# Cross attention over a long context: both batches' 32 heads in one pipeline, values read from DRAM by groups of four heads

## The chip, the cores and the metric

The program runs on one core of one Trainium2 chip. The metric is device time in microseconds (us) from start to end of one execution; less is better.

## What is computed

The program is a stack of twelve attention and feed-forward blocks on `x` of 2 batches x 256 tokens x 256 channels. Two of them, L0_xattn and L1_xattn, attend to a long context, `ctx_1024`, of 2 x 4096 x 256. Both have 16 heads of 16 channels and compute, per batch and head, softmax(q k^T / 4) v over all keys, then an output projection, and add the result to `x`:

```python
# L0_xattn: keys and values are the context rows as they are, and 256 projected rows of fside
q = x1 @ Wq + bq
k = concat([ctx, fside @ Wk + bk]);  v = concat([ctx, fside @ Wv + bv])      # 4352 rows each
# L1_xattn: keys and values are projections of the context
q = x1 @ w_q.T + b_q;  k = ctx @ w_k.T + b_k;  v = ctx @ w_v.T + b_v         # 4096 rows each
out = softmax(q @ k.T / 4) @ v @ Wo + bo
```

Scores are computed to float32 accuracy from bfloat16 products: q and k are each written as a sum of three bfloat16 parts, and six products of parts are stacked on 96 rows of one matmul. Three more rows carry the negated row maximum.

## The kernel before, in words

Every block is a row of *stages* (`stage`): in each, the five engines run their own instruction streams, ordered by semaphores, and all engines meet at a stage's end. `cross_attention` handles both blocks, `raw` for L0_xattn. It first loads weights and the context of batch 0 and clears a value tensor `V` of 128 x key tiles x 512 floats (32 columns for each head: 16 values, a 1 for the sum of weights, zeros). Then come `normalize`, and `store_parts` for the queries, which makes products in PSUM, splits each tile of 128 x 512 into three bfloat16 parts (ScalarE makes the first, VectorE the rest, ScalarE the second, VectorE the third) and sends them to a DRAM scratch tensor through SyncE's DMA queue.

A hardware loop `turns` runs twice, once for each batch: load the stacked queries `qS`; fill `V` (for L0 by GpSimd copies of the context, for L1 by 32 projected tiles in `gemms`); `store_parts` for the keys (L0: 16 tiles turned by TensorE and 2 projected; L1: 16 projected); `long_attention` for 16 heads; a small stage `kept` that copies the result. Within `long_attention` SyncE loads the keys of one head into one of three buffers `kst`, six pieces of 16 partitions and one row group of ones; the loads for head i are issued when the scores of head i-3 are done:

```python
for i in range(N):
    if i >= 3:
        sp.wait_ge(score_ready, (i - 2) * per_head)
    for dst, src in key_loads(i):
        sp.dma_start(dst, src).then_inc(keys[i % 3], 16)
    if i == 2:
        for dst, src in next_loads: ...           # the context of batch 1
```

TensorE's order is written out by hand: in units of up to four key tiles it interleaves products for maxima of a later head (`maximum`, `psA`), scores of this head (`score`, `psS`), and values (`values`, `psO`). VectorE takes row maxima (L593), and GpSimd splits the negated maxima into three bfloat16 parts (`split_maxima`, L409 to L412), which TensorE turns (`turn`, L554) and VectorE copies under the queries (L603). The first score of head h waits for that. ScalarE exponentiates (L651). The first maximum of head i waits for `keys[i % 3]`. A head has 9 units in L0 and 8 in L1. The maxima run one head and four units ahead of the scores, so a head's maxima are all taken some 8 us after the head before it began.

## Time and profile before

| | us |
|---|---|
| median of 3 runs (lowest, highest) | 3368.19 (3364.87, 3373.6) |
| the profiled execution's own time | 3367.49 |
| its span in the trace | 3365.6 |
| TensorE busy (matmul) | 2692.3, 80% |
| VectorE, ScalarE, GpSimd busy | 1671.1, 1130.9, 191.8 |
| L0_xattn, from its first load to the next block's | 15.38 to 676.95 |
| L1_xattn, the same | 1209.56 to 1868.08 |

The page of the profile gives busy time of each engine, forty slices of the span with the granted TensorE clock, DMA queues, and the costliest groups of instructions. "SPq" is SyncE issuing DMAs, so its times are those of issue. "Granted clock" is TensorE's, as a share of 2.4 GHz. In stretches ("windows") the DMA share is the mean busy share of 16 DMA engines; it is modelled and can pass 1.

### The profile page before, as it was taken

The numbers are of one execution on the slowest core, as the hardware profiler recorded it, in microseconds if no ns is written. First come the engines' busy times: TensorE is split into PE (matmuls) and PEld (weight loads), VectorE is DVE, ScalarE is ACT, GpSimd is POOL, SyncE is SP. The second block draws the span as 40 slices with busy tenths as digits, with TensorE's granted clock in tenths as the row PEclk, the third lists the DMA queues.
The fourth block names the chain that finished last, engine by engine and source line by source line (L and its number), as shares of the span: only waits on it lengthen the run. The fifth ranks groups of instructions, "written<-read, shape, count | busy, mean of one in ns | idle before, by whom it ended". The sixth has DMA issues, their size and how long they took to land. (4 is left out here: it accounts for less than half of the span.)

```text
span 3365.6 us, 40011 instructions
## 1 busy us (share of the span) xinstructions
PE 2692.3 (80%) x15192; PEld 1516.4 (45%) x15192; DVE 1671.1 (50%) x2588; ACT 1130.9 (34%) x2060; POOL 191.8 (6%) x362
## 2 busy tenths in 40 slices
PE   3799499878999967998798489596773759978777
PEld 2344244435555543445344255343222646747446
DVE  5677477422111136783686487333897223221423
ACT  2466366511111103773476145121321213312220
POOL 2000100000000000000000055000000000000000
PEclk8799699988999987999799656797776889978888
DMA  4632553121222125441642000100100331020200
GB/s 156 148 61 44 118 107 59 25 77 38 75 75 75 37 88 154 69 59 38 153 63 40 24 10 1 48 24 0 51 0 0 125 137 51 1 78 1 82 0 7
DMA packets 89495, 202.15 MB, mean 60 GB/s; under 512 B 10770, under 2 KB 66322, under 8 KB 78354
## 3 DMA queue, kind: packets, MB, share of 16 engines
q1 hardware_dynamic: 85566, 184.09, 22.1%
q10 hardware_dynamic: 3750, 15.65, 1.2%
q8 instruction: 115, 1.88, 0.2%
q14 instruction: 64, 0.52, 0.1%
HBM read 171.56 MB, written 28.15 MB: 59 GB/s over the span
## 5 line engine op out<-in xcount | busy, mean ns | idle before, releaser
L593 DVE TENSOR_REDUCE sta_parts<-sta_psA 128x1 f32<-128x1024 f32 x544 | 626.1, 1188 | 220.4 <-PE sta_psA L513 216.8
L651 ACT ACTIVATE sta_probs<-sta_psS 128x512 f32<-128x512 f32 x1056 | 575.8, 597 | 376.1 <-PE sta_psS L524 374.4
L513 PE MATMUL sta_psA<-L_xattna_kst,L_xattn_qS 99*128 99x512 bf16 x1088 | 312.4, 403 | 94.6 <-DMA L_xattna_kst<-ones_rows 76.9
L524 PE MATMUL sta_psS<-L_xattn_qS,L_xattna_kst 99*128 99x256 bf16 x2112 | 355.7, 280 | 17.4 <-ACT sta_probs L651 13.3
L530 PE MATMUL sta_psO<-sta_probs,L_xattn_V 128*32 128x256 f32 x4224 | 323.4, 387 | 0.0
L524 PEld LDWEIGHTS sta_psS<-L_xattn_qS,L_xattna_kst 99*128 99x128 bf16 x2112 | 165.7, 99 | 259.6 <-ACT sta_probs L651 174.4
L513 PEld LDWEIGHTS sta_psA<-L_xattna_kst,L_xattn_qS 99*128 99x128 bf16 x1088 | 99.9, 100 | 209.1 <-DMA L_xattna_kst<-ones_rows 93.0
L530 PEld LDWEIGHTS sta_psO<-sta_probs,L_xattn_V 128*32 128x32 f32 x4224 | 136.3, 109 | 90.9 <-issue 42.1
L1308 DVE TENSOR_TENSOR l0f_hT<-exp_psG,l0f_gel 128x512 f32<-128x512 f32 x72 | 49.8, 691 | 203.9 <-PE exp_psG L1277 203.9
L199 ACT ACT_TABLE_LOAD x14 | 18.0, 1283 | 370.2 <-PEq L59 370.2
L1293 ACT ACTIVATE l0f_gel<-exp_psA 128x512 f32<-128x512 f32 x72 | 43.0, 597 | 274.9 <-PE exp_psA L1274 274.9
L1873 PE MATMUL l2t_psY<-l2t_hc,top_consts_weights 128*128 128x512 f32 x128 | 93.7, 842 | 32.8 <-DVE l2t_hc L1909 32.6
L908 ACT ACTIVATE sht_probs<-sht_psS 128x768 f32<-128x768 f32 (+1 forms) x64 | 55.3, 863 | 155.6 <-PE sht_psS L752 99.4
L853 DVE TENSOR_REDUCE sht_Z<-sht_psM 128x2 f32<-128x512 f32 (+1 forms) x128 | 69.4, 586 | 38.3 <-PE sht_psM L745 37.6
L1274 PE MATMUL exp_psA<-l0f_xnT,grp_W 128*128 128x512 f32 x160 | 77.5, 607 | 10.1 <-PEq L78 6.3
L1880 ACT ACTIVATE l2t_decay<-l2s_delta,l2s_A 128x512 f32<-128x512 f32 x64 | 46.0, 721 | 110.0 <-DVE l2t_h L1905 110.0
L1905 DVE TENSOR_TENSOR_SCAN l2t_h<-l2t_decay,l2t_u 128x256 f32<-128x256 f32 x128 | 80.9, 674 | 0.0
L1277 PE MATMUL exp_psG<-l0f_xnT,grp_W 128*128 128x512 f32 x160 | 75.4, 593 | 0.0
L1313 DVE SCALAR_TENSOR_TENSOR top_X<-exp_psY,l0f_here,top_X 128x256 f32<-128x256 f32 x36 | 17.4, 484 | 114.5 <-PE exp_psY L1284 114.5
L250 PE MATMUL gem_banks<-3f_L_ffn_experts_weights,l3f_hT 128*128 128x256 f32 x288 | 64.3, 387 | 12.5 <-PEq L59 12.5
L1284 PE MATMUL exp_psY<-grp_W,l0f_hT 128*128 128x256 f32 x320 | 70.4, 381 | 4.3 <-DVE l0f_hT L1308 4.3
L1996 PE MATMUL l2e_psX<-l2f_place,l2f_xn 128*128 128x128 f32 x128 | 22.9, 353 | 62.2 <-DVE l2f_place L2058 62.2
(574 smaller groups left out, 4259.2 us busy)
## 6 DMA issues: line engine op xcount, KB each, us to landing
L_xattna_kst<-L_xattn_keys SPq DMA_DIRECT2D x192, 136.0 KB
L_xattn_keys<-prt_parts SPq DMA_DIRECT2D x64, 384.0 KB, 2.6
L_xattna_kst<-L_xattn_keys SPq DMA_DIRECT2D x192, 128.0 KB
grp_W<-in_W SPq DMA_DIRECT2D x15, 1024.0 KB, 7.1
l0f_W<-in_W SPq DMA_DIRECT2D x12, 1024.0 KB, 7.0
L_xattn_cx<-in_ctx SPq DMA_DIRECT2D x10, 1024.0 KB, 17.9
L_xattn_cxT<-in_ctxT SPq DMA_DIRECT2D x10, 1024.0 KB, 17.3
grp_W<-in_M SPq DMA_DIRECT2D x10, 1024.0 KB, 7.5
```

The lines of the kernel that those rows point to most:

```text
L250: last = nc.tensor.matmul(view(n), *term, start=i == 0, stop=i == len(terms) - 1)
L513: last = nc.tensor.matmul(psA[:, u % 2, col:col + rhs.shape[1]], lhsT, rhs, start=True, stop=True)
L524: last = nc.tensor.matmul(psS[:, at % 2, j * T:(j + 1) * T], lhsT, rhs, start=True, stop=True)
L530: last = nc.tensor.matmul(psO[32 * group:32 * group + 32, 0:T], v, probs[:, u % NP, col:col + T], start=first, stop=final)
L593: nc.vector.tensor_reduce(into(parts[:, u // n % 2]), view(psA[:, u % 2, :]), AX.X, ALU.max).then_inc(max_taken, 1)
L651: nc.scalar.activation(probs[:, u % NP, i * 512:(i + 1) * 512], psS[:, at % 2, :], ACT.Exp, scale=scale).then_inc(probs_ready, 1)
L853: last = nc.vector.tensor_reduce(Z[:, g % 2, t, 2 * (u % 2):2 * (u % 2) + 2, 16], psM[:, u % 2, :, at:at + w], AX.X, ALU.max, negate=True)
L1274: last = nc.tensor.matmul(psA[:, m % 2, :], W1[i][:, k, s], xnT[:, k, :], start=k == 0, stop=k == KC - 1)
L1277: last = nc.tensor.matmul(psG[:, m % 2, :], W2[i][:, k, s], xnT[:, k, :], start=k == 0, stop=k == KC - 1)
L1284: last = nc.tensor.matmul(psY[:, t, 0:C], hT[:, f, t * P:(t + 1) * P], W3[i][:, f, :], start=f == 0, stop=f == FC - 1)
L1873: nc.tensor.matmul(psY[:, m, :], K["ident"], hc[:, i % 3, :], start=s == 0, stop=s == NS - 1).then_inc(summed, 1)
L1905: nc.vector.tensor_tensor_scan(h[:, i % 2, c], decay[:, i % 3, c], u[:, i % 2, c], 0.0, ALU.mult, ALU.add).then_inc(states_ready, 1)
```

## The change

It does five things.

1. The loop over batches is gone. `long_attention` is called once for each block with 32 items, head h of batch b being item 16 b + h. Queries of both batches lie in `qS` at once, keys of both in one scratch tensor, and results go straight to `attT`; the stage `kept` is gone.
2. `V` is no longer a tensor for all heads. Three buffers of 128 x 32 x 128 floats hold the values of four heads each; SyncE loads group g+1 when it reaches head 4g, in the middle of its key loads. `values` waits for the buffer at the first unit of a group. For L0 the padded values are an input in DRAM (`ctxV`), laid out on the host; the clearing of `V` and GpSimd's copies are gone.
3. In L0 the keys need no turning: the context is also an input in transposed form. `store_parts` takes SBUF tiles directly as sources; before the attention it handles 2 query tiles, 4 tiles of fside keys of 256 columns, and only 8 of 32 context tiles (heads 0 to 7 of batch 0).
4. The other 24 context tiles are *blocks* inside `long_attention`: SyncE fetches two for each head, GpSimd splits them in four instructions each (`split_block`) after the maxima of that head, and SyncE stores them one or more heads later (`keep`). Key loads for heads 8 to 15, 16 to 23, 24 to 31 wait for 8, 16, 24 stored blocks.
5. In L1 everything is projected before the attention, for batch 0 and then batch 1: `store_parts` for queries and keys (with the context of batch 1 loaded meanwhile), then the new `store_values`, which projects 32 tiles, adds the bias into padded rows of 32 columns a head, and stores them to a DRAM scratch tensor, 1 MB for every four tiles. GpSimd clears the row buffers first.

The diff, cut to its core:

```diff
-def store_parts(nc, K, jobs, SLOTS=6, pool_engine=()):
+def store_parts(nc, K, jobs, SLOTS=6, loads=()):
+    MADE = sum(1 for job in jobs if isinstance(job[2], list))
+        def source(n):
+            m, w, terms = jobs[n][0:3]
+            return banks[0:m, n % RING, 0:w] if n < MADE else terms
...
             @block.sync
             def _(sp):
+                for dst, src in loads:
+                    sp.dma_start(dst, src).then_inc(loaded, 16)
                 for n, (m, w, _, _, dst) in enumerate(jobs):
...
-def long_attention(nc, K, items, outs, scale, key_loads, next_loads, lead=4):
+def long_attention(nc, K, items, outs, scale, key_loads, value_loads, blocks=(), blocks_before=None, lead=4):
...
+        SRC, DST = 6, 4
+            source = p.sb("source", [P, SRC, 512])
+            left = p.sb("left", [P, 512])
+            bparts = p.sb("bparts", [P, DST, 3, 512], BF16)
...
+                def fetch(j):
+                    for m in range(2 * j, min(2 * j + 2, len(blocks))):
+                        if m >= SRC:
+                            sp.wait_ge(block_split, m - SRC + 1)
+                        sp.dma_start(source[:, m % SRC, :], blocks[m][0]).then_inc(fetched[m % SRC], 16)
+
+                def keep(j):
+                    for m in range(2 * j, min(2 * j + 2, len(blocks))):
+                        sp.wait_ge(block_split, m + 1)
+                        sp.dma_start(blocks[m][1], bparts[:, m % DST, :, :]).then_inc(stored[m % DST], 16)
+
+                load_keys(0)
+                load_keys(1)
+                load_values(0)
+                fetch(0)
+                fetch(1)
+                load_keys(2)
+                load_values(1)
+                for i in range(3, N):
+                    keep(i - 3)
+                    sp.wait_ge(score_ready, (i - 2) * per_head)
+                    if blocks:
+                        for d in range(DST):
+                            sp.wait_ge(stored[d], 16 * len(range(d, blocks_before(i), DST)))
+                    load_keys(i)
+                    if i % GROUP == 0 and i // GROUP + 1 < N // GROUP:
+                        sp.wait_ge(probs_used, (i - GROUP) * n)
+                        load_values(i // GROUP + 1)
+                    fetch(i - 1)
...
                 def values(u):
+                    if u % (n * GROUP) == 0:
+                        g = u // (n * GROUP)
+                        pe.wait_ge(vals[g % 3], 16 * len(value_loads(g)) * (g // 3 + 1))
...
+                def split_block(m):
+                    first, second, third = (bparts[:, m % DST, i, :] for i in range(3))
+                    gp.wait_ge(fetched[m % SRC], 16 * (m // SRC + 1))
+                    if m >= DST:
+                        gp.wait_ge(stored[m % DST], 16 * (m // DST))
+                    step(nc.gpsimd.tensor_copy(first, source[:, m % SRC, :]))
+                    step(nc.gpsimd.tensor_tensor(left[:], source[:, m % SRC, :], first, ALU.subtract))
+                    step(nc.gpsimd.tensor_copy(second, left[:]))
+                    nc.gpsimd.tensor_tensor(third, left[:], second, ALU.subtract).then_inc(block_split, 1)
...
                         divide((h - 2) // GROUP - 1)
+                    for m in range(2 * h, min(2 * h + 2, len(blocks))):
+                        split_block(m)
...
+def store_values(nc, K, W, bias, xT, scratch, loads=()):
+    RING, SLOTS = 4, 3
+    BATCH = 4
+        rows = p.sb("rows", [P, SLOTS, BATCH, H, 32])
...
+                    nc.vector.tensor_tensor(rows[:, m % SLOTS, t % BATCH, :, 0:D], banks[:, t % RING, 0:C].rearrange("p (h d) -> p h d", h=H),
+                                            bias.rearrange("p (h d) -> p h d", h=H), ALU.add).then_inc(added, 1)
...
+                for m in range(NB):
+                    sp.wait_ge(added, (m + 1) * BATCH)
+                    for g in range(4):
+                        sp.dma_start(scratch[g, :, m * BATCH:(m + 1) * BATCH, :],
+                                     rows[:, m % SLOTS, :, 4 * g:4 * g + 4, :].rearrange("p t h d -> p t (h d)")).then_inc(stored[m % SLOTS], 16)
...
-        with turns(nc, B) as b:
...
+                load(nc, w.loads + context_loads(0))
+                normalize(nc, K, X, xn, xnT, 1e-5)
+                for b in range(B):
+                    store_parts(nc, K, (q_jobs if b == 0 else []) + [
...
+                         keys_at(b, m, n, 512)) for n in range(0, S, 512) for m in range(KC)], loads=context_loads(1) if b == 0 else ())
+                    store_values(nc, K, w["v"], w["bv"], cxT[b], scrv[b], queries if b == 0 else ())
...
+            V = [p1.sb(f"V{i}", [P, ST, P]) for i in range(3)]
...
+            blocks = [(context(b, k, n), keys_at(b, k, n, 512)) for b, k in ((0, 1), (1, 0), (1, 1)) for n in range(0, S, 512)] if raw else []
```

SyncE's DMAs in L0's attention, before: keys for the first heads (`kst0` to `kst2`), the context of batch 1, then keys alone.

```order
L498 DMA L0_xattna_kst1<-L0_xattn_keys 16x4352 x6
L498 DMA L0_xattna_kst2<-L0_xattn_keys 16x4352 x6
L501 DMA L0_xattn_cx<-in_ctx 128x2048 x4
L501 DMA L0_xattn_side<-in_fside 128x2x256
L498 DMA L0_xattna_kst0<-L0_xattn_keys 16x4352 [waits score_ready_729]
```

And in the changed kernel, where `sta474_source` holds fetched blocks and `sta474_bparts` split ones:

```order
L508 DMA L0_xattna_kst1<-L0_xattn_keys 16x4352 x6
L512 DMA L0_xattna_V0<-in_ctxV 128x4096
L518 DMA sta474_source<-in_ctxT 128x512 x4
L508 DMA L0_xattna_kst2<-L0_xattn_keys 16x4352 x6
L512 DMA L0_xattna_V1<-in_ctxV 128x4096
L523 DMA L0_xattn_keys<-sta474_bparts 128x3x512 [waits block_split_475] x2
L508 DMA L0_xattna_kst0<-L0_xattn_keys 16x4352 [waits stored2_475,stored1_475,stored3_475,stored0_475,score_ready_475]
L508 DMA L0_xattna_kst0<-L0_xattn_keys 16x4352 x5
L518 DMA sta474_source<-in_ctxT 128x512 x2
```

Stores of blocks now stand ahead of a head's key loads in the same queue, and values and fetches behind them.

GpSimd's rows in L0's attention, before, for one head (`sta728_neg` is the negated maximum):

```order
L409 CAST sta728_split<-sta728_neg 128x2
L410 TENSOR_TENSOR sta728_rest<-sta728_neg,sta728_split 128x2
L411 CAST sta728_split<-sta728_rest 128x2
L412 TENSOR_TENSOR sta728_split<-sta728_rest,sta728_split 128x2
```

And now:

```order
L417 TENSOR_TENSOR sta474_split<-sta474_rest,sta474_split 128x2
L723 CAST sta474_bparts<-sta474_source 128x512
L724 TENSOR_TENSOR sta474_left<-sta474_source,sta474_bparts 128x512
L725 CAST sta474_bparts<-sta474_left 128x512
L726 TENSOR_TENSOR sta474_bparts<-sta474_left,sta474_bparts 128x512
```

The last four stand there twice for each of heads 0 to 11, between the maxima of one head and of the next.

## Rows read from the trace of the kernel before

**Rows 1.** Page, busy time of each engine (share of the span) and instructions.

```profile
PE 2692.3 (80%) x15192; PEld 1516.4 (45%) x15192; DVE 1671.1 (50%) x2588; ACT 1130.9 (34%) x2060; POOL 191.8 (6%) x362
```

**Rows 2.** Stretches: us; PE, PEld, DVE, ACT, POOL busy; clock, DMA share, GB/s.

```profile
15.38:94.45 79.07, 31.83 (x100) 20.95 (x100) 42.79 (x61) 25.17 (x44) 14.34 (x6) 0.78 0.55 181
134.28:361.70 227.42, 204.73 (x1869) 97.20 (x1867) 155.97 (x162) 145.21 (x280) 13.72 (x60) 0.98 0.32 51
361.70:402.47 40.77, 21.38 (x80) 15.34 (x80) 25.57 (x38) 20.59 (x37) 8.25 (x4) 0.63 0.64 184
1549.20:1616.53 67.33, 57.11 (x192) 37.37 (x192) 35.29 (x64) 20.48 (x33) 0.00 (x0) 0.93 0.36 107
1616.53:1653.29 36.76, 25.98 (x112) 7.98 (x116) 23.27 (x23) 7.87 (x15) 1.54 (x8) 0.58 0.83 181
```

**Rows 3.** SyncE's issues of key loads in order of time: start, us, instructions.

```profile
94.45 3.12 SPq L498 DMA_DIRECT2D L_xattna_kst<-L_xattn_keys  x6
...
134.28 2.64 SPq L498 DMA_DIRECT2D L_xattna_kst<-L_xattn_keys  x6
...
304.55 3.77 SPq L498 DMA_DIRECT2D L_xattna_kst<-L_xattn_keys  x6
...
442.40 2.64 SPq L498 DMA_DIRECT2D L_xattna_kst<-L_xattn_keys  x6
...
1309.45 2.65 SPq L498 DMA_DIRECT2D L_xattna_kst<-L_xattn_keys  x6
...
1346.09 2.64 SPq L498 DMA_DIRECT2D L_xattna_kst<-L_xattn_keys  x6
...
1501.43 2.62 SPq L498 DMA_DIRECT2D L_xattna_kst<-L_xattn_keys  x6
...
1653.29 2.64 SPq L498 DMA_DIRECT2D L_xattna_kst<-L_xattn_keys  x6
```

**Rows 4.** Timeline of L0's first part, stages before the attention.

```profile
38.93 5.85 PE L337 MATMUL prt_banks<-L_xattnq_xnT,L_xattn_L_xattn_weights 128*128 128x512 f32 x8 [1.05 <-PEq L59]
...
46.21 1.46 DVE L365 TENSOR_TENSOR prt_parts<-prt_left,prt_parts 128x512 bf16<-128x512 f32 x2
...
81.16 0.68 DVE L365 TENSOR_TENSOR prt_parts<-prt_left,prt_parts 128x512 bf16<-128x512 f32 x1
...
82.55 0.68 DVE L365 TENSOR_TENSOR prt_parts<-prt_left,prt_parts 128x512 bf16<-128x512 f32 x1
...
90.50 0.98 DVE L365 TENSOR_TENSOR prt_parts<-prt_left,prt_parts 128x256 bf16<-128x256 f32 x2
```

**Rows 5.** Timeline of L1's stages before the attention.

```profile
1232.62 6.34 PE L337 MATMUL prt_banks<-L_xattnq_xnT,L_xattn_L_xattn_weights 128*128 128x512 f32 x8 [1.05 <-PEq L59]
...
1245.43 29.25 PE L250 MATMUL gem_banks<-L_xattn_L_xattn_weights,L_xattn_cxT 128*128 128x256 f32 x128 [6.47 <-PEq L59]
...
1275.46 27.70 PE L337 MATMUL prt_banks<-L_xattn_cxT,L_xattn_L_xattn_weights 128*128 128x512 f32 x64 [0.78 <-PEq L59]
```

**Rows 6.** Stretches: DMA at full share on large rows, key stores, query loads.

```profile
22.00:24.00 2.00, 0.00 (x0) 0.00 (x0) 2.00 (x1) 0.00 (x0) 0.00 (x0) 1.00 1.01 430
...
375.00:400.00 25.00, 13.70 (x53) 8.89 (x50) 22.58 (x34) 16.69 (x32) 4.39 (x2) 0.69 0.72 251
...
55.00:57.00 2.00, 1.88 (x5) 0.97 (x3) 0.51 (x2) 0.00 (x0) 0.00 (x0) 0.50 1.18 144
57.00:59.00 2.00, 0.00 (x0) 0.00 (x0) 0.34 (x1) 0.00 (x0) 0.00 (x0) 1.00 1.21 114
```

**Rows 7.** One key load in L0's attention: its issue, and TensorE's wait for it.

```profile
262.62 3.18 SPq L498 DMA_DIRECT2D L_xattna_kst<-L_xattn_keys  x6
...
271.18 0.61 PE L513 MATMUL sta_psA<-L_xattna_kst,L_xattn_qS 99*128 99x512 bf16 x2 [0.43 <-DMA L_xattna_kst<-ones_rows]
```

**Rows 8.** The same key load: DMA share and GB/s in stretches (columns as in rows 2).

```profile
268.00:270.00 2.00, 2.00 (x24) 0.96 (x23) 2.00 (x2) 1.17 (x3) 0.00 (x0) 1.00 0.45 57
270.00:272.00 2.00, 1.57 (x12) 0.93 (x12) 1.13 (x4) 1.09 (x2) 0.19 (x1) 1.00 0.00 0
```

**Rows 9.** GpSimd's groups: instruction, shape, count, busy us, mean ns; L1566's min/median/max.

```profile
L1047 POOL COPY L_xattn_V<-L_xattn_cx 128x2048 f32<-128x2048 f32 x8 | 16.5, 2063 | 59.4 <-POOLq L59 59.0
...
L1018 POOL MEMSET L_xattn_V<- 128x6144 f32 x1 | 5.2, 5217 | 484.0 <-PEq L59 484.0
...
L1566 POOL TENSOR_TENSOR hyp_D<-hyp_D,hyp_R x32: 1257/1712/1723, 1958.6 to 2063.0; 128x512 f32<-128x512 f32 x32
```

More of the change, by code:

```diff
@@ L371, in _ @@
                         dve.wait_ge(third_ready, n - 1)
-                    dst, src, first = left[0:m, n % 2, 0:w], banks[0:m, n % RING, 0:w], parts[0:m, n % SLOTS, 0, 0:w]
+                    dst, src, first = left[0:m, n % 2, 0:w], source(n), parts[0:m, n % SLOTS, 0, 0:w]
                     if bias is None:
@@ L393, in _ @@
                     sp.wait_ge(stored[i], 16 * len(range(i, len(jobs), SLOTS)))
+                if loads:
+                    sp.wait_ge(loaded, 16 * len(loads))
 def key_pieces(dst, scratch, h, cols):
@@ L487, in long_attention, with load_keys @@
                 (block, pool_step, max_product, score_ready, max_taken, max_ready, max_split, max_turned, shifted, probs_ready,
                  probs_used, o_copied, combined, n_copied, sums_ready, sums_read, inverted, out_ready,
-                 next_loaded, *keys):
+                 block_split, *more):
+            keys, vals, fetched, stored = more[0:3], more[3:6], more[6:6 + SRC], more[6 + SRC:]
             @block.sync
             def _(sp):
-                for i in range(N):
-                    if i >= 3:
-                        sp.wait_ge(score_ready, (i - 2) * per_head)
+                def load_keys(i):
@@ L1075, in lora_attention @@
+        add_to_residual(nc, K, X, w["o"], attT, 4, w["bo"])
 def lora_attention(nc, K, X, arrays, specs, own, ahead):
```

168 lines of the change are left out of this document (91 added, 77 removed).

## The prediction

> **What bounds the kernel now.** The page comes first. TensorE is busy 2692.3 us of 3365.6, but that is an average over twelve blocks [rows 1]; the change touches two of them, so I read stretches next. In the middle of L0's attention TensorE is busy 204.73 of 227.42 us at a clock of 0.98: nothing there is to be had unless its work shrinks, and it doesn't [rows 2]. Ahead of each attention it is different: in 15.38 to 94.45 TensorE works 31.83 of 79.07 us, and the second turn of the loop repeats such a stretch (361.70 to 402.47) and then one in which the new pipeline fills at a low clock (the row of L1's is 1616.53 to 1653.29, clock 0.58) [rows 2]. Third, the key-load issues serve as a ruler, since each is released by the scores of one head. L0 from 134.28 to 304.55 is 12 heads, 14.19 us each; L1 from 1346.09 to 1501.43 is 12 heads, 12.95 each [rows 3]. The same point of the two turns is 442.40 - 134.28 = 308.1 us apart in L0 and 1653.29 - 1346.09 = 307.2 in L1 [rows 3]. What exceeds 16 heads is what the loop's boundary costs: 308.1 - 227.1 = **81.0** in L0, 307.2 - 207.2 = **100.0** in L1.
>
> **The boundary.** One pipeline of 32 heads runs through it. In L0 nothing of the second turn's preparation is left between the heads (its blocks go to GpSimd, its side keys and values to the front): -81.0. In L1 the projections of batch 1 remain, only earlier: values 1275.46 - 1245.43 = 30.0 and keys 1309.45 - 1275.46 = 34.0 [rows 3, 5]. So -100.0 + 64.0 = -36.0. The small stage that copies results also goes, about a microsecond a turn by its four copies; I leave it out.
>
> **L0 before its first head.** The load shrinks from 6.03 MB (weights 1.57, context 4.19, fside 0.26) to 4.59 (weights 1.97, fside 0.52, half a context 2.10). At the 430 GB/s of a full stretch that is 3.3 us less [rows 6]. The clearing of `V` lay beside this load and gives nothing. `store_parts` now has 14 tiles in one stage: the first two end where they did, at 47.67, four of 256 columns take 1.3 each (my estimate, a little under the full ones), eight full ones 1.39 (82.55 - 81.16), giving 64.0; a stage needs 94.45 - 91.48 = 3.0 to drain and change [rows 3, 4]. Then the query load, which hides the side values' projection. It is 1.57 MB in place of 0.79. The rows show 114 to 144 GB/s at full share, thus 11 to 14 us; pieces are now 1 KB, so I take 11, with 3 for issue and landing: 14 [rows 6]. Keys of head 0 are issued at 64.0 - 3.3 + 3.0 + 14 = 77.7, not 94.45: **-16.8**.
>
> **L0 during its heads.** Three things are added, and each needs its cover named.
> - GpSimd, two blocks a head in heads 0 to 11. A copy of 512 elements costs 2063 / 4 = 0.52 us by the 2048-element copies; a subtraction of 128 x 512 costs between 1.26 (minimum) and 1.71 (median) [rows 9]. A block is 2 x 0.52 + 2 x (1.26 to 1.71) + 0.3 for semaphores = 3.9 to 4.8 us, two of them 7.7 to 9.5. With 1.1 for the maxima GpSimd is occupied at most 10.6 of 14.19: hidden by TensorE's head. Were the cover gone, the next head's maxima would be turned late and TensorE would wait.
> - The queue. The key load is the delicate one: issued at 262.62, its DMA ends before 270, and TensorE still waits 0.43 for it, until 271.18 [rows 7, 8]. There is no slack, so what stands ahead in the queue counts. Per head the keys use about 0.32 x 14.19 = 4.5 us of all engines by the share of the long stretch [rows 2]. Two stored blocks are 0.79 MB at 251 / 0.72 = 349 GB/s: 2.3 us; two fetches 0.52 MB at some 400: 1.3; a group of values, 16 KB a partition, 2.10 MB at 430: 4.9 [rows 6]. The worst heads (4, 8, 12) have all four: 13.0 of 14.19. They fit, so I charge 0. If a third more were needed, each of three heads would lose 3 to 4: bound 12.
> - SyncE waits for block m before it issues keys. GpSimd finishes the blocks of head i-3 well over half a head before the scores that SyncE waits for anyway: 0.
>
> A fetch behind a values load lands some 4 us after GpSimd wants it; with 9.5 us of work it still ends ahead of the next maxima. L0 comes to -81.0 - 16.8 = **-97.8**.
>
> **L1 before its first head.** Queries and keys in one stage: 12.8 (1232.62 to 1245.43) plus 34.0 becomes 9 for the queries, 16 tiles at 27.7 / 16 = 1.73, and 3 to drain, 39.7: -7.1 [rows 3, 5]. The 4.19 MB of batch 1 pass beside it in 10 us at 430 GB/s, before the first store is ready [rows 6].
> **Values are the uncertain term.** Before, 30.0 us a batch went into SBUF. Now each batch writes 8.39 MB to DRAM, in pieces of 512 B on the SBUF side, and no row shows such a store. Bounds: the key stores (1 KB pieces, same direction, all partitions) reach 349 GB/s, 24 us; the query loads (512 B pieces, but into 16 partitions) 114 / 1.21 to 144 / 1.18, about 108 GB/s, 78 us [rows 6]. The first row is nearer. If a 512 B piece cost as much as a 1 KB one, it would be 48 us; I take the middle of 24 and 48, 36. Batch 0 starts storing at 13 (the query load is ahead in the queue), batch 1 at 9 (GpSimd's clearing, 5.2 + 0.4, and four tiles); with 3 at the end 52 and 48, not 30 and 30: **+40** [rows 5, 9]. Ends: +22 where the projection itself (5.6 + 29.3 + 6 = 41) is the limit, +122 at 108 GB/s.
> In the heads only 2.10 MB each four heads is added, 4.9 us beside some 4.5 in 12.95: 0. L1 comes to -36.0 - 7.1 + 40 = **-3.1**.
>
> **Sum.** -97.8 - 3.1 = -100.9. Against the profiled execution's own 3367.49: **3266.6**. The median of the runs, 3368.19, is 0.7 higher, which I ignore.
>
> **Rivals.**
> A. The value stores hide completely behind the projection. For it: 24 us at the key stores' rate is below 29. Against: smaller pieces. +22 for +40 gives 3249. The Trainium skill ("DMA: Bandwidth & Descriptors", Specifications) puts the smallest transfer for line rate at 512 B, by which A would hold; no row of this trace shows a 512 B store. Chance 0.17.
> B. The value stores run at the query loads' 108 GB/s: +122 for +40 gives 3349; L1 alone would then be slower by 79. For it: the only 512 B pieces in the trace. Against: those go into 16 partitions, and the key loads of long rows into 16 partitions are slow as well (0.45 at 57 GB/s, 127 at full share), so it is the partitions, not the size [rows 8]. Chance 0.08.
> C. GpSimd becomes the bound in heads 0 to 11. It decides from 6.5 us a block (2 x 6.5 + 1.1 = 14.1); at 8 us the head takes 17.1, twelve heads lose 35: 3302. For it: the subtraction's time rose from 1.26 to 1.71 where other engines were at work [rows 9], and bfloat16 operands are in no row. Against: VectorE mostly reads PSUM in the attention. The Trainium skill ("GPSIMD Engine Reference", Key points) says that GpSimd shares its SBUF interfaces with VectorE and suffers beside instructions with two SBUF inputs; those are rare here. Chance 0.09.
> D. **Slower than before.** The values load, not the blocks, makes each following key load late. Place: TensorE's first maximum of a new head, where 0.43 us of waiting stands already [rows 7]. If 2.10 MB moved at 108 GB/s instead of 430, a load would take 19.4 us; with 4.5 for keys it overruns a head by 9.7 in L0 and 11.0 in L1, six times each: +124, 3391. It decides from about 17.5 us a load (8.4 late, twelve times, eats the 101). Against: rows of 16 KB to all partitions are the case that ran at 430 [rows 6]. Chance 0.04.
>
> **How the numbers follow.** My forecast has 0.60, A 0.17, C 0.09, B 0.08, D 0.04; 0.02 is left for gains and losses that cancel. Low end 3236: A, with the query load 3 faster and a copy stage and some head time gained. High end 3305: 512 B pieces at 48 us (+24, 3291), the queue's bound of 12, and C. This leaves out B and D and a little more, 0.15. A measurement of this kernel tells 0.3%, 10 us, from no change. Only D is slower: 0.04. No change: 0.02. Faster: 0.94.
>
> **What would show it.** Right: the ruler shows 32 equal heads of 14.2 and 31 of 12.9 or 13.0 with no gap; L0's first key load at about 78; GpSimd blocks of 4 to 5 us; key waits still under 1 us a head. The value stage in L1 of 48 to 52 us tells forecast (48 to 52) from A (41) and B (90). Wrong: heads 0 to 11 of L0 longer than the rest (C), heads after 4, 8, 12 and so on longer, with waits on `kst` (D). The blocks other than these two should keep their times to a microsecond.

## The result, and the profile after

The changed kernel takes 3243.95 us (median of 4 runs, 3240.88 to 3249.93), the kernel before 3366.53 (3362.82 to 3373.6): ratio 0.9638, 95% interval 0.9624 to 0.9652. So it is faster, by 122.6 us and not by 100.9; the forecast of 3266.6 was 22.7 too slow, and the time lies inside the stated range of 3236 to 3305. The profiled execution has 3249.93 us of its own and a span of 3247.9, 117.7 shorter than the span before; the sums below are of spans. The page's span and busy line, the second to be set beside [rows 1]:

```profile
span 3247.9 us, 39531 instructions
...
PE 2635.5 (81%) x15052; PEld 1492.4 (46%) x15056; DVE 1610.8 (50%) x2516; ACT 1100.9 (34%) x2010; POOL 260.0 (8%) x450
```

The busy line says little: TensorE has 140 instructions fewer. What it waited for lies in the stretches (columns as in [rows 2]): L0 ahead of its first key load, 16 heads of L0, its next 12, L1 ahead of its first key load, 16 heads of L1.

```profile
15.38:79.67 64.29, 21.97 (x48) 11.11 (x48) 23.37 (x47) 16.72 (x32) 0.00 (x0) 0.81 0.62 170
119.87:350.53 230.66, 218.63 (x1993) 105.37 (x1992) 177.12 (x179) 153.34 (x296) 89.13 (x152) 1.00 0.70 158
350.53:522.81 172.28, 164.22 (x1495) 78.99 (x1494) 134.03 (x135) 115.08 (x222) 11.52 (x51) 1.00 0.48 86
1122.04:1304.64 182.60, 128.44 (x400) 81.50 (x400) 76.58 (x147) 43.16 (x72) 11.28 (x4) 0.85 0.74 229
1341.11:1547.75 206.64, 199.43 (x1868) 98.88 (x1872) 164.40 (x164) 146.74 (x281) 14.62 (x67) 1.00 0.54 105
```

The ruler of [rows 3], SyncE's issues of key loads (heads 0, 3, 15, 19 and 31 of L0 and the first issue of the next block; heads 3 and 19 of L1):

```profile
79.67 2.65 SPq L508 DMA_DIRECT2D L_xattna_kst<-L_xattn_keys  x6
...
119.87 2.64 SPq L508 DMA_DIRECT2D L_xattna_kst<-L_xattn_keys  x6
...
293.01 2.62 SPq L508 DMA_DIRECT2D L_xattna_kst<-L_xattn_keys  x6
...
350.53 2.62 SPq L508 DMA_DIRECT2D L_xattna_kst<-L_xattn_keys  x6
...
522.81 2.62 SPq L508 DMA_DIRECT2D L_xattna_kst<-L_xattn_keys  x6
...
587.21 0.83 SPq L121 DMA_DIRECT2D l0a_L_attn_weights<-in_L_attn  x2
...
1341.11 2.62 SPq L508 DMA_DIRECT2D L_xattna_kst<-L_xattn_keys  x6
...
1547.75 4.00 SPq L508 DMA_DIRECT2D L_xattna_kst<-L_xattn_keys  x6
```

No gap is left between the batches. The same point of the two batches was 308.1 us apart in L0 and 307.2 in L1; heads 3 and 19 are now 230.7 and 206.6 apart. L0 as a whole went from 661.6 to 571.8 (-89.7), L1 from 658.5 to 639.0 (-19.5), and everything else changed by -8.4.

Where L1 spent its 182.6 us ahead of the attention, TensorE's runs of matmuls in each stage show (start, us; in brackets the idle time before and its releaser; L343 is `store_parts`, L1069 `store_values`):

```profile
1151.40 27.63 PE L343 MATMUL prt_banks<-L_xattnq_cxT,L_xattn_L_xattn_weights 128*128 128x512 f32 x64
1185.43 5.23 PE L1069 MATMUL val_banks<-L_xattn_L_xattn_weights,L_xattnq_cxT 128*128 128x256 f32 x16 [6.40 <-PEq L59]
...
1228.66 29.82 PE L343 MATMUL prt_banks<-L_xattnq_cxT,L_xattn_L_xattn_weights 128*128 128x512 f32 x64 [7.97 <-PEq L59]
1265.01 6.38 PE L1069 MATMUL val_banks<-L_xattn_L_xattn_weights,L_xattnq_cxT 128*128 128x256 f32 x16 [6.53 <-PEq L59]
1272.03 24.44 PE L1069 MATMUL val_banks<-L_xattn_L_xattn_weights,L_xattnq_cxT 128*128 128x256 f32 x112 [0.64 <-DVE val_rows L1080]
```

The value stages begin at 1185.43 and 1265.01 and end where the next stage begins, at 1228.66 and at the first key load, 1304.64: 43.2 and 39.6 us. In the first, VectorE waited 6.2 us for stored rows (us in total, times, longest); in the second never:

```profile
DVE val_rows L1080 <- DMA L_xattn_values<-val_rows: 6.2, 2, 4.6
```

While batch 1's rows were stored, the DMA engines moved 276 GB/s at a share of 0.93, thus 276 / 0.93 = 297 at full share:

```profile
1273.00:1301.00 28.00, 23.47 (x109) 20.33 (x107) 11.89 (x28) 0.00 (x0) 0.00 (x0) 1.00 0.93 276
```

GpSimd's instructions on the blocks (min/median/max ns, first and last start):

```profile
L723 POOL CAST sta_bparts<-sta_source x24: 611/611/612, 101.4 to 269.7; 128x512 bf16<-128x512 f32 x24
L724 POOL TENSOR_TENSOR sta_left<-sta_source,sta_bparts x24: 1153/1158/1165, 102.1 to 270.4; 128x512 f32<-128x512 f32 x24
L725 POOL CAST sta_bparts<-sta_left x24: 610/611/612, 103.3 to 271.6; 128x512 bf16<-128x512 f32 x24
L726 POOL TENSOR_TENSOR sta_bparts<-sta_left,sta_bparts x24: 1153/1157/1165, 104.0 to 272.3; 128x512 bf16<-128x512 f32 x24
```

A block is 3.8 us from the start of one to the start of the next.

### The profile page after: what moved, and what is told of

Its sections match the earlier page's. It is cut to its first block and busy times, and to the rows that moved or that the text cites. A ratio compares the mean times of both kernels' runs of the same rounds, so it can differ in the third digit from the quotient of the medians.

```text
span 3247.9 us, 39531 instructions
## 1 busy us (share of the span) xinstructions
PE 2635.5 (81%) x15052; PEld 1492.4 (46%) x15056; DVE 1610.8 (50%) x2516; ACT 1100.9 (34%) x2010; POOL 260.0 (8%) x450
## 5 line engine op out<-in xcount | busy, mean ns | idle before, releaser
L553 PE MATMUL sta_psA<-L_xattna_kst,L_xattn_qS 99*128 99x512 bf16 x1088 | 297.5, 388 | 69.3 <-DMA L_xattna_kst<-ones_rows 53.7
L573 PE MATMUL sta_psO<-sta_probs,L_xattna_V 128*32 128x256 f32 x4096 | 303.7, 386 | 0.0
L573 PEld LDWEIGHTS sta_psO<-sta_probs,L_xattna_V 128*32 128x32 f32 x4096 | 131.9, 109 | 83.0 <-issue 34.6
L1364 PE MATMUL exp_psA<-l0f_xnT,grp_W 128*128 128x512 f32 x160 | 77.5, 607 | 10.2 <-PEq L78 6.3
L414 POOL CAST sta_split<-sta_neg 128x2 bf16<-128x2 f32 x64 | 12.1, 190 | 811.9 <-issue 477.8
L1069 PE MATMUL val_banks<-L_xattn_L_xattn_weights,L_xattnq_cxT 128*128 128x256 f32 x256 | 62.4, 408 | 17.2 <-PEq L59 12.9
## 6 DMA issues: line engine op xcount, KB each, us to landing
L_xattna_V<-in_ctxV SPq DMA_DIRECT2D x8, 2048.0 KB, 11.5
```

What stands on the lines that cost most here:

```text
L553: last = nc.tensor.matmul(psA[:, u % 2, col:col + rhs.shape[1]], lhsT, rhs, start=True, stop=True)
L573: last = nc.tensor.matmul(psO[32 * group:32 * group + 32, 0:T], v, probs[:, u % NP, col:col + T], start=first, stop=final)
L1069: last = nc.tensor.matmul(banks[:, t % RING, 0:C], xT[:, k, t * P:(t + 1) * P], W[:, k, 0:C], start=k == 0, stop=k == KC - 1)
L1364: last = nc.tensor.matmul(psA[:, m % 2, :], W1[i][:, k, s], xnT[:, k, :], start=k == 0, stop=k == KC - 1)
```

## The experiments

The marks used below are issues of SyncE, counted from the first load of L1's block: the first store of values of batch 0, of keys of batch 1, of values of batch 1, and the first key load. The last mark lies between 180.4 and 182.6 in the eight traces in which nothing ahead of it in L1 differs, so less than 2 us there says nothing.

| kernel | time, us | ratio to before | values b0 | keys b1 | values b1 | key load |
|---|---|---|---|---|---|---|
| changed | 3243.95 | 0.9638 | 71.2 | 114.5 | 151.0 | 182.6 |
| changed, again | 3246.54 | 0.9645 (0.9629 to 0.966) | 70.8 | 113.4 | 149.8 | 181.4 |
| 2 KB pieces | 3239.05 | 0.9628 (0.9615 to 0.9641) | 71.0 | 110.1 | 146.5 | 175.2 |
| cleared once | 3246.61 | 0.9648 (0.9629 to 0.9666) | 68.9 | 114.0 | 149.4 | 181.2 |
| queries later | 3247.39 | 0.9655 (0.9634 to 0.9676) | 70.9 | 110.3 | 146.7 | 178.1 |
| stored twice | 3302.56 | 0.981 (0.9795 to 0.9825) | 70.8 | 144.2 | 180.6 | 241.3 |
| all four edits | 3214.24 | 0.955 (0.9537 to 0.9563) | 68.6 | 106.2 | 140.3 | 168.9 |

**Is the join of the pipelines the gain?** All preparation stays in front, but the 32 heads run as two pipelines.

```diff
-            long_attention(nc, K, items, [attT[:, g, b * T:(b + 1) * T] for b in range(B) for g in range(4)], 0.25,
...
+            for b in range(B):
+                long_attention(nc, K, items[b * H:(b + 1) * H], [attT[:, g, b * T:(b + 1) * T] for g in range(4)], 0.25,
...
+                               blocks if b == 0 else (), lambda i: i // 8 * 8)
```

> The changed kernel with the 32 heads as two pipelines of 16, one after the other, with all preparation of both batches still ahead of the first (and all 24 blocks in L0's first pipeline): only the join of the pipelines is undone. Theory 1, from the boundary's terms: L0's boundary was 78.6 us, of which the second turn's preparation is 40.8 (361.70 to 402.47), so the drain, stage change and fill at a low clock cost 37.8; in L1 100.0 - 64.0 = 36.0. So 3244 + 74 = 3318. Rival, most of a fill is done beside the drain of the pipeline ahead or hangs on loads that now come early (keys and values are ready in DRAM): 15 us each, 3274.

3323.97 us, ratio 0.9875 (0.9859 to 0.9892). SyncE's issues at L0's join (heads 15, 16 and 19):

```profile
292.41 2.62 SPq L508 DMA_DIRECT2D L_xattna_kst<-L_xattn_keys  x6
...
341.44 2.62 SPq L508 DMA_DIRECT2D L_xattna_kst<-L_xattn_keys  x6
...
381.92 2.62 SPq L508 DMA_DIRECT2D L_xattna_kst<-L_xattn_keys  x6
```

Heads 15 to 19 take 89.5 us, in the changed kernel 350.53 - 293.01 = 57.5: the join costs 32.0 in L0, and by the same reckoning 28.7 in L1. That is twice the rival's 15 and somewhat under the 37.8 and 36 of theory 1. The total rose by 80 (the span by 72.5): 60.7 are the joins, 6.5 lie between the two blocks and 9.6 behind L1, in blocks that no edit touched (last experiment), and the rest of the two blocks became some 4 shorter. So of L0's boundary of 81 about 41 was preparation and 32 the join. The other 8 lie at the batch's end: from VectorE's last reciprocal to the next batch's first load the kernel before takes 11.2 us (350.48 to 361.70), with the stage `kept` and a first stage of the next turn in between, and this run 3.1 (338.34 to 341.44). The 41 are not all moved under the attention: in L0 the turning of tiles and the filling of `V` are gone, since the host lays the inputs out, and no run separates that from the blocks on GpSimd.

**What do the blocks on GpSimd save, and what do they cost?** All 32 tiles are split ahead of the attention.

```diff
-                first = p1.sb("first", [P, S])
+                first = p1.sb("first", [P, 4, S])
...
+                            + [(P, 512, first[:, 2 * b + k, n:n + 512], None, keys_at(b, k, n, 512)) for b in range(B) for k in range(KC) for n in range(0, S, 512)])
```

> The changed kernel, but all 32 context tiles of L0 are split ahead of the attention on ScalarE and VectorE, none on GpSimd beside it. By the terms of the prediction: 6.3 MB more in the first load at 430 GB/s, 14.6 us, and 24 tiles at 1.39 us, 33.4 us, so the first key load is issued at 79.7 + 48 = 128; the twelve heads that had blocks beside them give back the 2.9 us by which they were longer: time 3244 + 45 = 3289. Rival 1, the blocks beside the attention cost more than the 2.9 us (queue, GpSimd's SBUF accesses in all heads): the heads of L0 fall by more than 3 us of 173 in the twelve, and the time is under 3280. Rival 2, the load overlaps or the tiles go faster in a long stage (nothing to fill): under 33 us for the tiles.

3296.6 us, ratio 0.979 (0.9773 to 0.9806). The first key load and those of heads 3 and 15:

```profile
127.60 2.62 SPq L508 DMA_DIRECT2D L_xattna_kst<-L_xattn_keys  x6
...
167.11 2.62 SPq L508 DMA_DIRECT2D L_xattna_kst<-L_xattn_keys  x6
...
339.26 2.62 SPq L508 DMA_DIRECT2D L_xattna_kst<-L_xattn_keys  x6
```

The preparation grew by 127.60 - 79.67 = 47.9, as the two prices say (48), so nothing of it was hidden (rival 2). Heads 3 to 15 take 172.2 against 173.1 with the blocks. That difference of 1 us is one pair of traces: in the five other traces with the same L0 (changed again and the four edits of L1 alone) these heads take 173.6 to 175.8, so the 24 blocks cost between 1 and 4 us beside the attention. Rival 1 falls by the time, which is far above 3280, though in the heads its 3 us is not excluded. My reading that the blocks account for the 2.9 us by which those heads are longer than before the change is not shown: without blocks they are still 1.9 longer than the 170.3 of [rows 3]. The rest of the rise is again behind L1 (+6.6).

**How near is GpSimd to being the bound?** Its instructions on a block are repeated (with the same results). My edit made nine of four, not eight, so a block became 8.8 us and not the 7.5 of the text.

```diff
+                    for _ in range(2):
+                        step(nc.gpsimd.tensor_copy(first, source[:, m % SRC, :]))
...
+                        step(nc.gpsimd.tensor_tensor(third, left[:], second, ALU.subtract))
                     nc.gpsimd.tensor_tensor(third, left[:], second, ALU.subtract).then_inc(block_split, 1)
```

> The changed kernel with every step of a GpSimd block done twice (the same values written again): 7.5 us a block in place of 3.8. Theory 1, the prediction's (GpSimd bounds a head from 6.5 us a block): 2 x 7.5 + 1.1 = 16.1 plus a wait of about 0.4 us for the maxima, against a head of 14.1 to 14.4: twelve heads become 16.3 to 16.5 us, +24 to +28, time 3268 to 3272, and heads 12 to 31 stay as they are. Rival 1, GpSimd slows the other engines by its accesses to SBUF and not by its own length: heads lose in proportion to its busy time even below the bound, thus as much more as twelve heads lost before (2.9 us): 3247 plus the excess. Rival 2, the maxima are split a head ahead, so there is a head of slack which two blocks too long eat slowly: +10 to +15.

3301.11 us, ratio 0.9805 (0.9788 to 0.9822). What TensorE waited for in the twelve heads (us in total, times, longest), and the stretch:

```profile
PE sta_psM L597 <- POOL sta_split L417: 36.5, 11, 4.3
```

```profile
121.66:345.55 223.89, 183.78 (x1495) 84.78 (x1494) 131.95 (x133) 115.01 (x222) 190.27 (x247) 0.89 0.60 137
```

223.9 against 173.1, +50.8, or 18.7 us a head. The rule of rival C, two blocks and 1.1 for the maxima, gives 2 x 8.8 + 1.1 = 18.7. The rule is right, the number expected was wrong by the ninth instruction. The wait stands where C said, at the turning of the maxima, and is 36.5 us. The rest comes with the clock, 0.89 in place of 1.00: the same 1495 matmuls were busy 183.8 us against 163.9 in the changed kernel's heads 3 to 15. Rival 2, a head of slack eaten slowly, would have cost 10 to 15 us in all and falls. So does rival 1, a loss in proportion to GpSimd's busy time: at 3.8 us a block GpSimd needs 8.7 of 14.4, and all 24 blocks cost at most 4 us.

**Are the key loads late?** In the changed kernel TensorE waited for keys in about half of the heads, at most 1.3 us each (L0's heads, then L1's):

```profile
PE sta_psA L553 <- DMA L_xattna_kst<-ones_rows: 10.8, 15, 1.2
PE sta_psA L553 <- DVE sta_parts L636: 7.0, 6, 1.2
...
PE sta_psA L553 <- DMA L_xattna_kst<-ones_rows: 10.5, 17, 1.3
```

In the twelve heads from 3 to 15 of L0 these waits went from 3.3 us in the kernel before to 6.0 in the changed one (5.0 in the run without blocks), and 2.7 more is what the 2.9 of longer heads asks for:

```profile
PE sta_psA L513 <- DMA L_xattna_kst<-ones_rows: 3.3, 7, 0.6
PE sta_psA L553 <- DMA L_xattna_kst<-ones_rows: 6.0, 7, 1.2
```

A fourth key buffer lets SyncE ask for keys one head earlier.

```diff
+                load_keys(3)
                 for i in range(3, N):
...
-                    load_keys(i)
+                        load_keys(i + 1)
...
-            kst = [p1.sb(f"kst{i}", [PLAIN_ROWS, KT * P], BF16) for i in range(3)]
+            kst = [p1.sb(f"kst{i}", [PLAIN_ROWS, KT * P], BF16) for i in range(4)]
```

> The changed kernel with four key buffers instead of three, so that the keys of head i+1 are asked for where those of head i were. In the changed kernel TensorE's first maximum of a head waits for keys some 0.4 to 0.6 us, 53.7 us in the whole program. Theory 1, the key load is a real limit of every head (it is issued at the end of a head's scores and lands just too late): the wait goes to under 0.1 us a head, a head becomes shorter by up to 0.5 us, 58 heads: the time falls by 20 to 30 us to about 3215 to 3225. The 2.9 us that twelve heads of L0 lost beside the blocks goes too. Theory 2, the wait only stands in for another one (the ring of probabilities, the maxima's reduction by VectorE) that would end just as late: kst disappears as a releaser but another takes its place, time within 5 us of 3244.

3221.8 us, ratio 0.958 (0.9565 to 0.9595): 22 us less (20 by the ratios), and theory 1 holds. The traces put it in the heads: L0 is 12.0 us shorter and L1 from its first key load on 10.6. In L0's heads the waits for keys are gone and nothing stands in their place; the waits for VectorE's maxima are as before:

```profile
PE sta_psA L555 <- DVE sta_parts L638: 7.0, 6, 1.2
```

```profile
119.39:343.06 223.67, 218.36 (x1993) 104.99 (x1992) 176.35 (x179) 153.34 (x296) 88.88 (x152) 1.00 0.73 165
1324.97:1524.70 199.73, 198.43 (x1868) 99.22 (x1871) 164.49 (x164) 146.73 (x281) 14.54 (x67) 1.00 0.55 108
```

16 heads take 223.7 and 199.7 in place of 230.7 and 206.6, with the blocks running as before; heads of one kind are now equal to 0.1 us.

**Does a longer values load make keys late?** Each values load gets a second one of half its size, into a buffer that nothing reads.

```diff
-                           lambda g: [(V[g % 3][:], scrv[g // 4, g % 4])],
+                           lambda g: [(V[g % 3][:], scrv[g // 4, g % 4]), (V2[g % 3][:], scrv[g // 4, g % 4][:, 0:ST // 2])],
```

> The changed kernel with every load of a group of values followed by a second one of half its size (1.05 MB) into a buffer that nothing reads: 1.5 times the traffic of values in both attentions. Theory 1: the load stands in the queue behind the keys of one head and is done 10 us before those of the next are asked for, so nothing becomes later: time within 4 us of 3244, and the wait for keys per head as it was. Theory 2 (rival D of the prediction, in small): a values load delays what stands behind it; after heads 4, 8, 12 and so on, where fetches of blocks (L0) and the next keys follow, TensorE's wait for keys grows by up to 2.4 us, twelve times: up to +29, with the worst in L0's heads 4, 8 and 12, where GpSimd's blocks start later and end after the next maxima.

3266.81 us, ratio 0.9699 (0.9681 to 0.9716), 20 to 23 us slower. It is theory 2's place, but twice its size in three heads and little elsewhere: the heads behind L0's values loads take 19.4, 20.2 and 18.5 where they took 14.5, 14.7 and 14.2. These, behind heads 4, 8 and 12, are also the ones with fetches and stores of blocks in the queue. In L1 no blocks run, and with the same longer values loads all heads from 3 to 31 lose only 3.5 us together. SyncE's queue behind head 4, then TensorE's wait:

```profile
138.33 0.36 SPq L512 DMA_DIRECT2D L_xattna_V<-in_ctxV  x1
138.73 0.44 SPq L512 DMA_DIRECT2D L_xattna_W<-in_ctxV  x1
139.22 0.91 SPq L518 DMA_DIRECT2D sta_source<-in_ctxT  x2
...
149.66 0.32 SPq L508 DMA_DIRECT2D L_xattna_kst<-L_xattn_keys  x1
```

```profile
161.30 1.03 PE L553 MATMUL sta_psA<-L_xattna_kst,L_xattn_qS 99*128 99x512 bf16 x2 [3.52 <-DMA L_xattna_kst<-ones_rows]
```

```profile
159.00:161.00 2.00, 0.00 (x0) 0.00 (x0) 0.00 (x0) 0.00 (x0) 1.77 (x4) 0.69 0.94 178
161.00:163.00 2.00, 1.70 (x6) 0.73 (x6) 0.63 (x1) 0.14 (x1) 1.61 (x4) 0.50 1.04 366
163.00:165.00 2.00, 2.00 (x18) 0.62 (x18) 0.59 (x1) 0.94 (x2) 1.86 (x3) 0.50 0.25 88
165.00:167.00 2.00, 2.00 (x12) 1.06 (x9) 0.17 (x1) 1.09 (x2) 1.85 (x3) 0.60 0.00 0
```

The keys issued at 149.66 were there for TensorE only at 161.3; the DMA share was between 0.85 and 1.17 in every stretch of 2 us from 150 to 160. TensorE waited 3.52 us, in which its clock fell, and worked for some four more at 0.50 (1.2 GHz). In the changed kernel the same head had waited 0.96 us already. So 2.56 us more of waiting made this head 4.9 longer: the other 2.35 are its 125 matmuls, busy 15.88 us in place of 13.53. The Trainium skill ("TensorE: Matmul & The Clock Gate", Part 1) has the throttled clock as the default, which activity releases; the rows agree, with 0.69 and 0.50 around the wait and 1.00 again from 167.

The same load with the fourth key buffer tells whether the late keys are all of it, or the late fetches too. The edit is the two above together (with two spare buffers).

> Four key buffers, and the values loads at 1.5 times their bytes as before. Theory 1 (the harm of the longer values load is that keys, asked for just in time, land 3.5 us late, and that TensorE's clock falls to 0.50 while it waits): a head of slack takes it all, no wait for keys in the heads, every head of 13.70 or 15.04 as with four buffers alone: 3222 to 3226. Theory 2 (the harm is in the late fetches, which make GpSimd's blocks and then its split of the maxima late): heads 4, 8 and 12 of L0 stay 3 to 5 us longer, 3232 to 3240.

3226.46 us, ratio 0.9586 (0.9573 to 0.9599), within the 3222 to 3226 of theory 1 but for half a us. The extra load costs 4.7 us and not 20 to 23; one head of slack takes the rest, and theory 2 falls. Of the twelve heads with blocks only two are longer, by 0.6 and 0.7.

**What do the value stores cost?** First their price where they are surely the bound: every batch of rows is stored twice, the second time into another tensor.

```diff
-                    for g in range(4):
-                        sp.dma_start(scratch[g, :, m * BATCH:(m + 1) * BATCH, :],
...
+                    for g in range(8):
+                        sp.dma_start((scratch, again)[g // 4][g % 4, :, m * BATCH:(m + 1) * BATCH, :],
```

> The changed kernel, but each batch of value rows in L1 is stored twice, into two tensors in DRAM, so that the stores of 512 B pieces (16.8 MB a batch) certainly set the length of both value stages and their price can be read. At the 297 GB/s read at full share in the changed kernel: 56.4 us of stores, behind 8 us to the first and 3.3 after the last, 68 us for batch 1 in place of 39.6, and batch 0 71 in place of 43.3: 3300. At the key stores' 349 GB/s 59, 3283. At the 36 us for 8.39 MB that the prediction took, 83 us a stage, 3330.

```profile
1300.00:1356.00 56.00, 24.28 (x101) 19.71 (x100) 9.64 (x26) 0.00 (x0) 0.00 (x0) 0.80 0.96 286
```

From the first store of batch 1 to the first key load 60.7 us pass, in place of 31.6: the second 8.39 MB cost 29.1. Batch 0's stage grew by 30.0, and the whole by 56 to 59, to 3302.56 as the 297 GB/s said. So 8.39 MB in 512 B pieces are 29 to 30 us, where the prediction took 36.

Then the piece is changed, by another order of the row buffer:

```diff
-        rows = p.sb("rows", [P, SLOTS, BATCH, H, 32])
+        rows = p.sb("rows", [P, SLOTS, 4, BATCH, 4, 32])
```

> The changed kernel with the value rows of L1 laid out in SBUF so that a store's piece is 2 KB and not 512 B; nothing else. Theory 1, the stores are hidden (batch 1: projection 29 us behind 5.6 us of clearing; stores 28 us in all): the value stage of batch 1 stays at 39.6 us, that of batch 0 loses at most the 4 us that it waits behind the query load: time 3240 to 3244. Theory 2, that of the prediction, the pieces of 512 B set the stage's length: batch 1 falls to 34 to 36 and batch 0 to 36 to 38, time 3233 to 3236. The rate of the stores at full share tells it directly: 297 GB/s now, 349 if 2 KB pieces go as the key stores do, no change if the size of the piece does not matter.

```profile
1271.48:1297.23 25.75, 23.47 (x109) 20.33 (x107) 11.89 (x28) 0.00 (x0) 0.00 (x0) 1.00 0.79 300
```

300 GB/s at a share of 0.79, thus 380 at full share, against 297 of 512 B pieces. L1's first key load comes 7.4 us earlier, 4.3 in batch 0 and 2.9 at the end of batch 1. Neither theory is quite right. VectorE never waits for stored rows in batch 1 with either piece, so the projection sets the pace; but with small pieces the last stores trail it by 2.9 us more. The whole time, 3239.05, can't be told from 3243.95 by its interval; the last mark, 175.2 against 180.4 to 182.6, can.

**Is it the query load that holds batch 0's stores?** The query load is moved into the parts stage of batch 1.

```diff
-                         keys_at(b, m, n, 512)) for n in range(0, S, 512) for m in range(KC)], loads=context_loads(1) if b == 0 else ())
-                    store_values(nc, K, w["v"], w["bv"], cxT[b], scrv[b], queries if b == 0 else ())
+                         keys_at(b, m, n, 512)) for n in range(0, S, 512) for m in range(KC)], loads=context_loads(1) if b == 0 else queries)
+                    store_values(nc, K, w["v"], w["bv"], cxT[b], scrv[b])
```

> The changed kernel, but the query load of L1 (1.57 MB) is put in the queue of the key-and-parts stage of batch 1 and not ahead of the value stores of batch 0. Theory 1 (it is what makes VectorE wait 7 us for stored rows in batch 0's value stage): that stage falls from 43.3 to 39.6 us like batch 1's; the parts stage of batch 1 takes it in with 0 to 4 us more, since it has six slots and a low share of DMA: time 3240 to 3244. Theory 2 (the stores need the time anyway): batch 0's stage stays above 42, and batch 1's parts stage becomes longer: 3244 to 3252.

Theory 1 holds: from values b0 to keys b1 it takes 39.4 us in place of 43.4, and from keys b1 to values b1 36.4 as before, so the parts stage takes the load in for nothing. L1's preparation is 178.1 in place of 180.4 to 182.6, though the whole time (3247.39, runs from 3239 to 3259) doesn't show it.

**Does GpSimd's clearing ahead of each value stage cost its 5.6 us?** The row buffer is cleared once, beside the first load of the block.

```diff
-        rows = p.sb("rows", [P, SLOTS, BATCH, H, 32])
...
+                rows = p1.sb("rows", [P, 3, 4, H, 32])
+                load(nc, w.loads + context_loads(0), None, [lambda: nc.gpsimd.memset(rows[:], 0.0), lambda: nc.gpsimd.memset(rows[:, :, :, :, D], 1.0)])
```

> The changed kernel, but the row buffer of L1's value stages is allocated once and cleared once, beside the load at the start of the block, not at the start of each value stage. Theory 1 (the projection and the 5.6 us of clearing ahead of it set the stage): batch 1 falls from 39.6 to about 34 us, batch 0 by less, 0 to 2, since it waits for stores behind the query load: time 3236 to 3238. Theory 2 (the stores set it): they start 5.6 us earlier as well but need 28.2 us at 297 GB/s, so batch 1 ends at 3.5 + 28.2 + 3 = 35 at best, and stands at 39 if the stores were already what ended last.

A miss: L1's first key load comes at 181.2, within the 180.4 to 182.6 of unchanged preparation, and the time is 3246.61. The first stores do come earlier, by 2.3 us in batch 0 and, counted from the keys' first store, by 1.0 in batch 1, but in batch 0 VectorE then waits longer for stored rows (7.5 us in place of 6.2). For batch 1, VectorE's first additions in this run show why:

```profile
1264.67 0.42 DVE L1072 TENSOR_TENSOR L_xattnq_rows<-val_banks,L_xattn_L_xattn_weights 128x256 f32<-128x256 f32 x1 [5.72 <-PE val_banks L1062]
1266.37 0.42 DVE L1072 TENSOR_TENSOR L_xattnq_rows<-val_banks,L_xattn_L_xattn_weights 128x256 f32<-128x256 f32 x1 [1.28 <-PE val_banks L1062]
...
1269.15 0.42 DVE L1072 TENSOR_TENSOR L_xattnq_rows<-val_banks,L_xattn_L_xattn_weights 128x256 f32<-128x256 f32 x1 [0.65 <-PE val_banks L1062]
```

The first three tiles come 1.7 us apart, the fourth 1.1 behind and the later ones 0.86 apart: TensorE starts the stage at its lower clock (0.50 from 1262 to 1268), behind 6.5 us of idling. In the changed kernel it computed its first four tiles (6.38 us, at 0.50 as well) beside the clearing. The clearing was nearly hidden by work that is slow anyway.

**All four edits together.**

> The changed kernel with four edits: four key buffers, value rows in 2 KB pieces, rows cleared once beside the load, query load in the parts stage of batch 1. By the single runs: 22 us for the key buffers. In L1 ahead of the first key load 2 KB pieces gave 7.4, the clearing 1.4 and the query load 4.5, but the 4.3 that batch 0's value stage can lose is in two of these, so 9 together: 3244 - 31 = 3213. If the gains simply add (-35) 3209; if the value stages come to stand on the projection at the low clock of their start (nothing but 29 us of matmuls and 6 of start), the key buffers and 6 us are left: 3216.

3214.24 us, ratio 0.955 (0.9537 to 0.9563): 32 us under the changed kernel measured beside it, 150 under the kernel before, and the fastest version here. L1's preparation lost 13.7 us (at least 11.5 against the unchanged marks), more than the 9 expected: batch 0's value stage, from its first store on, takes 37.6 us in place of 43.4, and VectorE waits for stored rows in neither batch. That it profits from the clearing once the query load is out of its way is the likely reason; no run has these two edits alone.

**What belongs to the run and not to the kernel?** The changed kernel once more, unedited.

> The changed kernel itself once more, beside the three others. Both theories: 3244 within 3 us, so that the others stand against it on the same chip; the part of the program behind L1's attention at 1487 us, as in the first profile of it, if that value belongs to the kernel, or at another of the values that have been seen (1484, 1494, 1497) if it belongs to the run.

3246.54 us, 2.6 more than the first time. The part of the program behind L1 (before, changed, changed again):

```profile
1868.10:3365.60 1497.50, 1121.80 (x4992) 695.60 (x4992) 700.73 (x1400) 363.69 (x640) 93.41 (x71) 0.79 0.10 36
```

```profile
1761.02:3247.90 1486.88, 1112.48 (x4988) 691.57 (x4992) 700.22 (x1400) 363.57 (x640) 93.43 (x71) 0.79 0.10 36
```

```profile
1756.90:3240.30 1483.40, 1106.12 (x4988) 687.16 (x4992) 700.62 (x1400) 363.39 (x640) 93.39 (x71) 0.80 0.10 36
```

The same instructions, the same work on DVE, ACT and POOL, but 15.7 us between the longest and the shortest of TensorE's sums. In the twelve traces of these experiments the part takes 1483 to 1489 in ten, and 1493.5 and 1496.5 in the runs with 32 tiles in front and with two pipelines. Since one kernel has shown 1483.4 and 1486.9, 3.5 us belong to the run. Whether the 10 between 1487 and 1497 come from where in time a program reaches these blocks, or by chance, stays open.

## Why the prediction was right, and where its terms were off

Against -100.9 the spans show -117.7. The time fell into the range, and the two large terms of L0 hold for the reasons given. In L1 it was rival A, with its chance of 0.17, that happened and not the forecast's middle value, and errors of both signs partly cancel in the sum.

- **The boundary of L0, -81.0: right.** The issues of head 3 in the two batches stand 77.5 us nearer, and the missing 3.5 is the heads' (two points on). The split shows its parts: 41 of preparation, 32 of joining, 8 at the batch's end, where the prediction had put about a microsecond of copies.
- **L0 before its first head, -16.8: measured -14.8** (79.67 against 94.45), 2 us long somewhere in the load, the 14 tiles and the query load. Its prices for a tile and for the load give 48 us for the 24 tiles left out, and the run that puts them back shows 47.9.
- **L0 during its heads, 0 with a bound of 12: measured about +6.** Heads 3 to 19 take 230.7 where [rows 3] gave 227.1, 3.6 more; the next 12 take 1.8 more, ramp and end 0.4 each; in five other traces heads 3 to 19 take 231.0 to 233.1. The step that failed is "They fit, so I charge 0": a queue that has room for its bytes still delivers keys later when they share it. The text had seen that there was no slack, in the wait of 0.43 us [rows 7], and did not price it. Its own sign, key waits under 1 us, was missed too: the longest were 1.2 and 1.3. With a fourth buffer the heads (223.7) fall below those of before.
- **GpSimd, 3.9 to 4.8 us a block: 3.8.** bfloat16 results cost no more than float32 ones, and with VectorE busy for three quarters of the time a subtraction took 1.16 us throughout, below the 1.26 to 1.71 of [rows 9]. Rival C's rule for a head (two blocks and 1.1) is borne out by the 8.8 us blocks; where between 3.8 and 8.8 the loss begins no run shows.
- **The value stores, +40: measured +22.8** (43.2 and 39.6 where each batch had 30.0). This is the term that was mis-sized, in its middle step: "I take the middle of 24 and 48, 36" for 8.39 MB. They cost 29 to 30. Then the projection covers them, which is rival A. By the prediction's own sign (a value stage of 48 to 52 for the forecast, 41 for A) the stages of 43.2 and 39.6 are A's. A's mechanism happened in batch 1 but for the last stores, while batch 0 still waited for stores behind the query load; its +22 is the measured size, and its time, 3249, is nearer than the forecast. The Trainium skill ("DMA: Bandwidth & Descriptors", Specifications) has line rate from 512 B on, which I named with A: for these stores the runs disagree, with 297 GB/s for 512 B and 380 for 2 KB, but for the outcome 297 was enough.
- **The other terms of L1.** Query and key stages 40.6 and 36.4 against 39.7 and 34.0: +3. Its boundary and heads together gave some 2 us more than the 36. All of L1: -19.5 for -3.1.
- **Outside the two blocks, 0: measured -8.4** (+2.2 between them, -10.6 behind). "The other blocks should keep their times to a microsecond" was wrong. The changed kernel's second trace has +0.0 and -14.1, so some microseconds of this belong to the run.
- Rival B (108 GB/s) fell, and so did D as stated: after the values loads no head of the changed kernel was slower by more than a microsecond. But D's place is real and near: where blocks are fetched and stored as well, half a load more makes TensorE wait 3.5 us.

So the direction and the two large terms of L0 stood on sound rows, and the value stores and the key loads were the two steps that failed. Of the 22.7 us by which the median was missed, L1 is 16.4 (its value stores 17.2), the other blocks are 8.4, and L0 takes 8.1 back (its heads 6.2); the last 6.0 are the distance from the profiled execution, 3249.93, to the median, 3243.95.

## What to carry to other kernels

Add up small waits that come back head after head: 32 waits of at most 1.3 us were 21 us here, and one more buffer gave 22 back, more than the three edits of the stages together. Price a transfer against what runs beside it before pricing it alone, and ask what the engine would be doing at the start of a stage anyway: the clearing beside TensorE's slow first tiles cost almost nothing. Read a small edit by the marks of its own stage, and know how far those marks move when nothing is edited (2 us here), for in a long program the untouched blocks move by 3 to 10 us.

## What the runs showed of the hardware

- Stores from all partitions: 297 GB/s at full share in pieces of 512 B, 380 in pieces of 2 KB, beside the same matmuls.
- A wait of 3.5 us on TensorE in the middle of dense work was followed by some four microseconds at the lower of its two clocks. Against a wait of 0.96 in the same head it cost 4.9 in all.
- GpSimd: 0.61 us for a 128x512 copy from float32 to bfloat16 and 1.16 for a subtraction, with float32 or bfloat16 results alike, the same to 1% in all 24 blocks beside a VectorE that was busy for three quarters of the time.
- The same instructions behind L1 took 1483.4 to 1497.5 us in three traces; VectorE's, ScalarE's and GpSimd's busy times agreed within 0.6 us, TensorE's differed by 15.7.
